# A two-layer graph network: the second layer norm and the last product put two steps later, the statistics aggregated earlier within a step, and each PSUM bank of a seed copied on its own

## The reference

```
h  = max(layernorm(x), 0)
mask = adj > 0
hm[b,j] = sum_k mask[b,j,k] * relu(h[b,j] @ W1a + (h[b,j] - h[b,k]) @ W1b + b1)
x  = x + hm @ W2 + deg * b2
h  = max(layernorm(x), 0)
x  = x + (adj @ h) @ W^T
```

## Time and profile before

| | |
|---|---|
| median of 3 runs | 913.4 us |
| profiled execution | 911.69 us, span 909.7 us |
| TensorE busy | 842.6 us, 93% |
| VectorE busy | 851.5 us, 94% |
| ScalarE busy | 761.9 us, 84% |
| GpSimd busy | 614.1 us, 68% |
| mean granted TensorE clock | 0.994 |

### The profile page before, as it was taken

One profiled execution on the slowest core, in us unless ns is written; L12 is line 12 of the kernel. 1 busy time (PEld: TensorE's weight loads), 2 busy tenths in 40 slices (PEclk: granted clock), 3 DMA queues, 4 the chain that ended last, 5 costly groups with the idle time before them and its releaser, 6 DMA issues.

```text
span 909.7 us, 26109 instructions
## 1 busy us (share of the span) xinstructions
PE 842.6 (93%) x8242; PEld 718.0 (79%) x8243; DVE 851.5 (94%) x2908; ACT 761.9 (84%) x1728; POOL 614.1 (68%) x1164
## 2 busy tenths in 40 slices
PE   3768999999999999999999999999999999999995
PEld 1447888888888888888888888888888888888884
DVE  6989999999999999999999999999999999999994
ACT  4858888888888888888888888888888888888883
POOL 0956677667766776777677667766776677667763
PEclk9999999999999999999999999999999999999998
DMA  9700000000000000000000000000000000000000
GB/s 344 272 1 2 14 13 19 19 19 8 19 19 19 14 19 20 10 16 19 19 13 20 18 19 8 19 19 19 14 19 20 19 7 19 19 19 14 13 8 15
DMA packets 26699, 27.50 MB, mean 30 GB/s; under 512 B 3520, under 2 KB 24512, under 8 KB 25536
## 3 DMA queue, kind: packets, MB, share of 16 engines
q1 hardware_dynamic: 25488, 25.37, 8.2%
q10 hardware_dynamic: 1072, 0.43, 0.2%
HBM read 21.59 MB, written 4.19 MB: 28 GB/s over the span
## 4 chain that ended last, share of the span: by engine, by line
DVE 52%; PE 19%; issue 16%; ACT 9%; DMA 1%; POOL 1%; SPq 0%; DVEq 0%; ACTq 0%; POOLq 0%
DVE acc L808 31%; PE ring L400 10%; DVE onehot_space L794 7%; ACT ring L561 5%; DVE onehot_row L851 4%; DVE PQ L725 3%; PE prep L465 2%; PE prep L457 2%; DVE stats L865 2%; ACT row_space L604 1%; DVE x_all L861 1%; DMA x_all<-x_nbf_dram 1%; PE prep L463 1%; DVE mv L836 1%; DVE owner L845 1%
## 5 line engine op out<-in xcount | busy, mean ns | idle before, releaser
L808 DVE SCALAR_TENSOR_TENSOR acc<-ring,acc 128x384 f32<-128x384 f32 x896 | 490.3, 547 | 27.7 <-PE ring L400 26.8
L561 ACT COPY ring<-P 128x768 f32<-128x768 f32 x512 | 403.9, 811 | 59.0 <-DVE acc L808 47.7
L400 PE MATMUL ring<-PQ,onehot_space 128*128 128x192 f16 x4096 | 412.5, 247 | 32.5 <-ACT ring L561 19.9
L400 PEld LDWEIGHTS ring<-PQ,onehot_space 128*128 128x128 f16 x4096 | 319.6, 98 | 97.4 <-ACT ring L561 50.0
L918 POOL TENSOR_TENSOR row_space<-row_space 128x192 f32<-128x192 f32 x256 | 151.8, 593 | 125.7 <-ACT row_space L604 115.6
L904 POOL TENSOR_SCALAR start<-P,spare 128x192 f32<-128x192 f32 x128 | 120.0, 938 | 96.5 <-ACT P L618 95.7
L794 DVE TENSOR_SCALAR onehot_space<-mask_all 128x512 f16<-128x512 f16 x512 | 155.1, 305 | 0.0
L566 ACT ACTIVATE h<-x_all,shift,rstd 128x64 f32<-128x64 f32 x128 | 55.5, 434 | 60.0 <-POOL shift L936 60.0
L428 PE MATMUL ring<-PQ,owner 128*128 128x384 f16 (+1 forms) x512 | 93.9, 306 | 0.0
L400 PE MATMUL ring<-PQ,onehot_row 128*128 128x192 f16 x768 | 84.3, 246 | 1.6 <-DVE onehot_row L851 1.6
L604 ACT ACTIVATE row_space<-ring 128x576 f32<-128x576 f32 x128 | 82.4, 644 | 0.7 <-PE ring L400 0.7
(11 more groups left out here) (138 smaller groups left out, 1434.0 us busy)
## 6 DMA issues: line engine op xcount, KB each, us to landing
onehot_space<-adj_kbj_dram SPq DMA_DIRECT2D x8, 1024.0 KB, 17.8
adj_again<-adj_kbj_dram SPq DMA_DIRECT2D x128, 64.0 KB, 2.0
x_all<-x_nbf_dram SPq DMA_DIRECT2D x8, 512.0 KB, 18.5
out_dram<-x_all SPq DMA_DIRECT2D x32, 128.0 KB, 1.9
consts<-consts_dram SPq DMA_DIRECT2D x1, 192.0 KB, 2.5
scratch<-w1a_dram ACTq DMA_DIRECT2D x2, 48.0 KB, 4.2
scratch<-w1b_dram ACTq DMA_DIRECT2D x2, 48.0 KB, 6.9
scratch<-b_dram ACTq DMA_DIRECT2D x1, 96.0 KB, 10.0
```

The source lines that it names most:

```text
L400: last = nc.tensor.matmul(to, hot(s), parts[:, part, H:2 * H], start=False, stop=(part == 1), skip_group_check=True)
L561: return nc.scalar.copy(slots[to], src.unsqueeze(1).unsqueeze(1).broadcast_to([N, BANKS, PER_BANK, H]))
L808: return nc.vector.scalar_tensor_tensor(sums, slots[to][:, bank_], 0.0, start[:, :, :] if first else sums, ALU.max, ALU.subtract if first ...
```

## The change

Five things are changed.

- Layer 1's normalisation: `norm2` is gone. At the end of every step b (place `i == 4`) ScalarE normalises graph b-5, so the first graph of a pair at an odd step and the second at the next even step, one step later each than the statistics' step, or more. `h2` gets a second copy for each pair.
- The aggregation of a pair (L500) goes from odd step b for b-5 to odd step b for b-7, and the last product and addition (L468, L872) from b-6 to b-8 at even steps. `TAIL` becomes 7, and the counts of `transposes` and `mixes` follow. SyncE's reload waits for the aggregation two steps later.
- `bn_aggr` (L836) is issued after the first bank of chunk 0 and ahead of the one-hots, no longer after the second bank.
- The seed is two copies of 128x384, one for each bank, each with its own increment of `seeded`. The first waits for `half_summed` of the chunk that held the place, the second for `summed`.
- TensorE waits for `seeded` ahead of each bank's four products.

```diff
-            return (u - 5) % BODY, (b - 5) // BODY if isinstance(b, int) else t - 1 if u < 5 else t
+            return (u - 7) % BODY, (b - 7) // BODY if isinstance(b, int) else t - 1 if u < 7 else t
...
-                    sp.wait_ge(transposed, transposes(b + 5))
+                    sp.wait_ge(transposed, transposes(b + 7))
...
-                            pe.wait_ge(seeded, b * REGULAR + i + 1)
                             for bank_ in range(BANKS):
+                                pe.wait_ge(seeded, (b * REGULAR + i) * BANKS + bank_ + 1)
...
-                        if u % 2 and exists(b - 7):
-                            pe.wait_ge(y_ready, pairs(b, u, t, -7))
+                        if u % 2 and exists(b - 9):
+                            pe.wait_ge(y_ready, pairs(b, u, t, -9))
...
-                        if u % 2 and exists(b - 5):
-                            pe.wait_ge(h2_ready, b - 3)
+                        if u % 2 and exists(b - 7):
+                            pe.wait_ge(h2_ready, b - 5)
...
-            def seed(to, src):
+            def seed(to, src, bank_):
...
-                return nc.scalar.copy(slots[to], src.unsqueeze(1).unsqueeze(1).broadcast_to([N, BANKS, PER_BANK, H]))
+                return nc.scalar.copy(slots[to][:, bank_], src.unsqueeze(1).broadcast_to([N, PER_BANK, H]))
...
-                        if i in (0, 1) and exists(b - 1):
-                            act.wait_ge(summed, b * REGULAR - 1 + i)
...
-                        if i == 3:
-                            act.wait_ge(summed, b * REGULAR + 1)
-                        seed(place(u, i), P[:, u % 2, :]).then_inc(seeded, 1)
+                        for bank_, consumed in enumerate((half_summed, summed)):
+                            if i in (0, 1) and exists(b - 1):
+                                act.wait_ge(consumed, b * REGULAR - 1 + i)
+                            if i == 3:
+                                act.wait_ge(consumed, b * REGULAR + 1)
+                            seed(place(u, i), P[:, u % 2, :], bank_).then_inc(seeded, 1)
...
-                    if i == 1 and u % 2 and exists(b - 5):
-                        norm2(b, u, t, 1)
...
-                    if i == 4 and u % 2 == 0 and exists(b - 4):
-
-                        wait_apart(act, norm2_ready, pairs(b, u, t, -4))
-                        if exists(b - 6):
-                            act.wait_ge(transposed, transposes(b - 1))
-                        norm2(b, u, t, 0)
+                    if i == 4 and exists(b - 5):
+
+                        wait_apart(act, norm2_ready, pairs(b, u, t, -5 if u % 2 else -6))
+                        if exists(b - 9):
+                            act.wait_ge(transposed, transposes(b - 2 if u % 2 else b - 3))
+                        k, g = (u - 5) // 2 % 2, (u - 5) % 2
+                        nc.scalar.activation(h2[:, k, 2 * g, :], x_all[:, b - 5, :], ACT.Relu, bias=shift2[:, k, g:g + 1],
+                                             scale=rstd2[:, k, g:g + 1]).then_inc(h2_ready, 1)
...
                         consume(u, place(u, i), 0, i == 0).then_inc(half_summed, 1)
+                    if i == 0 and u % 2 == 0 and exists(b - 4):
+                        wait_apart(dve, stats2_ready, pairs(b, u, t, -4))
+                        for g in range(2):
+                            last = nc.vector.bn_aggr(mv[:, (u - 4) // 2 % 2, g, :], stats2[:, g, :])
+                        last.then_inc(mv_ready, 1)
                     if i < REGULAR:
                         prepare(b, u, i)
...
-                    if i == 4 and u % 2 == 0 and exists(b - 6):
+                    if i == 4 and u % 2 == 0 and exists(b - 8):
```

More of the change, by code:

```diff
@@ L161, in gnn_kernel @@
         shift2 = sb("shift2", [N, 2, 2])
-        h2 = sb("h2", [N, 3, F])
-        h2_padded = (h2[:, 0:2, :], h2[:, 1:3, :])
+        h2 = sb("h2", [N, 2, 3, F])
+        h2_padded = [(h2[:, k, 0:2, :], h2[:, k, 1:3, :]) for k in range(2)]
         ring = ctx.enter_context(nc.psum_tensor("ring", [N, RING, BANKS, 512], F32))
@@ L250, in gnn_kernel @@
         stored = sem("stored")
-        HEAD, TAIL = 3, 5
+        HEAD, TAIL = 3, 7
         LATE = PARTS - 1
@@ L295, in agg_at @@
         def agg_at(b, u, t):
-            return (u - 5) % BODY, (b - 5) // BODY if isinstance(b, int) else t - 1 if u < 5 else t
+            return (u - 7) % BODY, (b - 7) // BODY if isinstance(b, int) else t - 1 if u < 7 else t
         def transposes(step):
-            return step + 2 if isinstance(step, int) and step > B + 1 else step + 3
+            return B + 4 + (step - B - 1) // 2 if isinstance(step, int) and step > B + 1 else step + 3
         def mixes(step):
-            return step + 1 if isinstance(step, int) and step > B + 2 else step + 2
+            return B + 4 + (step - B - 2) // 2 if isinstance(step, int) and step > B + 2 else step + 2
         def pairs(b, u, t, d):
@@ L465, in step @@
                                 last = nc.tensor.matmul(out_ps[:, g, :], hmT[g], w2a[:, :], start=False, stop=True, skip_group_check=True)
-                        if u % 2 == 0 and exists(b - 6):
+                        if u % 2 == 0 and exists(b - 8):
                             pe.wait_ge(even_T_ready, pairs(b, u, t, -2))
@@ L499, in step @@
                                 pe.wait_ge(adj_again_in[at + g], times * 16 + 16)
-                                last = nc.tensor.matmul(agg_ps, h2_padded[g], adj_again[:, at + g, :], start=(g == 0), stop=(g == 1))
+                                last = nc.tensor.matmul(agg_ps, h2_padded[(u - 7) // 2 % 2][g], adj_again[:, at + g, :], start=(g == 0), stop=(g == 1))
                         if last:
@@ L587, in step @@
                         nc.scalar.copy(h1T[:, :], h1T_ps).then_inc(h1T_ready, 1)
-                    if i == 0 and u % 2 == 0 and (exists(b - 2) or exists(b - 6)):
+                    if i == 0 and u % 2 == 0 and (exists(b - 2) or exists(b - 8)):
                         act.wait_ge(transposed, transposes(b - 1))
-                        if exists(b - 4) or exists(b - 8):
+                        if exists(b - 4) or exists(b - 10):
                             act.wait_ge(mixed, mixes(b - 1))
-                        parts = slice(0 if exists(b - 2) else 1, 2 if exists(b - 6) else 1)
+                        parts = slice(0 if exists(b - 2) else 1, 2 if exists(b - 8) else 1)
                         nc.scalar.copy(sums_T[:, parts, :], sums_T_ps[:, parts, :]).then_inc(even_T_ready, 1)
@@ L638, in step @@
                             wait_apart(act, loop_summed, first + k + 1)
-                            seed(place(u, CHUNKS), P[:, u % 2, :]).then_inc(loop_seeded, 1)
+                            seed(place(u, CHUNKS), P[:, u % 2, :], 0)
+                            seed(place(u, CHUNKS), P[:, u % 2, :], 1).then_inc(loop_seeded, 1)
                         wait_apart(act, loop_summed, first + n + 1)
@@ L673, in _ @@
             nc.vector.memset(ones_h[:, :], 1.0)
-            nc.vector.memset(h2[:, 1, :], 0.0)
+            nc.vector.memset(h2[:, :, 1, :], 0.0)
             nc.vector.memset(row_space[:, 0, 0, H:H + F], 0.0)
@@ L832, in step @@
                         consume(u, place(u, i), 1, False).then_inc(summed, 1)
-                    if i == 0 and u % 2 == 0 and exists(b - 4):
-                        wait_apart(dve, stats2_ready, pairs(b, u, t, -4))
-                        for g in range(2):
-                            last = nc.vector.bn_aggr(mv[:, (u - 4) // 2 % 2, g, :], stats2[:, g, :])
-                        last.then_inc(mv_ready, 1)
                     if i == 0 and exists(b + 1):
@@ L870, in step @@
                             dve.wait_ge(p_ready, b + 2)
-                        pair = bass.ds(b - 6, 2)
+                        pair = bass.ds(b - 8, 2)
                         nc.vector.tensor_tensor(x_all[:, pair, :], x_all[:, pair, :], out_ps, ALU.add).then_inc(y_ready, 1)
```

4 lines of the change are left out of this document (removed).

## The result

The changed kernel takes 863.4 us, the median of 4 runs (858.9 to 867.0), beside 913.3 (912.8 to 913.5) for the one before: a ratio of 0.945, 95% interval 0.941 to 0.950. In a second set of runs it took 866.1 (863.4 to 870.3), beside 912.5. The forecast was 881.5 with a range from 867 to 905: the sign was right, the size too small by about a third (32 us of 50). The kernel's own times now spread over 8 us, where those of before lay within 1 us (within 2 us in the later sets of seven runs).

What follows compares the result with a forecast made beforehand. VectorE was taken as the bound, waiting for the odd graph's chunk 2: 911.7 - 32.6 + 0.7 = 879.8, plus 1.7 for the median, 881.5 us. Own range 868 to 895; 867 to 905 with rival 1 and some of 3.

Steps and rivals of the forecast that it cites:

- VectorE bounds the kernel, and its wait for the odd graph's chunk 2 is the gain: VectorE, 96.02 of 100 us busy, is the bound; its 0.44 us wait for TensorE's gather there can be given back.
- Rival 1: Seeds and gathers: the wait is shortened, not ended, only 0.21 a pair gained, 13.4 us, giving 899; chance 0.13.
- rival 2: ScalarE becomes the bound because half seeds don't overlap: slower, +26 us at the upper end, 940; chance 0.06.
- rival 4: Nothing changes: the gather waits for something else than seeds, or the wait only moves; 913 to 914, chance 0.03.
- VectorE stands still in one place worth naming, so a pair gives 0.51, 32.6 us in all: VectorE ahead of the odd graph's chunk 2: ending this one wait gives 0.51 in each of 64 pairs.
- Half seeds alone 0.43 at chunk 2, the move 0.21: TensorE's gathers: chunk 1's 0.43 earlier by half seeds, 0.21 more without waiting for chunk 2's seed; chunk 2's 0.64 earlier.
- The split's cost: ScalarE: splitting a seed costs about 0.005 us each, 0.04 a pair, up to 0.27 each; hidden at the low end.
- TensorE's waits, the aggregation, SyncE: TensorE's four more waits a graph, VectorE's earlier aggregation and SyncE's later reload: taken to cost or gain nothing.
- The end, +0.7: Last steps: +1.1 for a longer last round against at least 0.33 saved; net +0.7, bounds -0.5 and +2.3.
- VectorE and GpSimd, no change in the middle: VectorE's fp16 instructions lengthened by GpSimd: no net change taken, two meetings more or less (13 us) as range.
- rival 3: VectorE and GpSimd meet more often: eight meetings +26 us, 907, or 932 by the skill's rule; chance 0.06, half slower.
- The median is 1.7 above the profiled execution: Whole kernel: 1.7 us added to the 879.8 forecast for the profiled execution to get the median, 881.5.

Runs made afterwards that it cites:

- e9_no_reads_before: Kernel before the change, GpSimd's wide instructions in the graph loop (all but the 64-column ones) replaced by one- or two-element powers, their results left out: 887.9 us.
- e3_no_aggr: Changed kernel with the statistics aggregation back behind the second bank of chunk 0: 867.2 us, beside 866.1 for the changed kernel in the same set.
- e4_again: Changed kernel, unedited, run and traced once more: 866.1 us.
- e2_move: Kernel before with everything of the change but the half seeds, their waits, TensorE's waits for them and the earlier aggregation: 905.3 us, ratio 0.993.
- e8_bias_odd: Changed kernel with GpSimd's bias and its addition moved from the even to the odd step: 923.5 us, ratio 1.012.
- e1_split: Kernel before with only the two half seeds, their two waits and TensorE's wait for each bank: 871.5 us, ratio 0.955.

## Why the prediction was wrong

- *VectorE bounds the kernel, and its wait for the odd graph's chunk 2 is the gain*: right, as far as it goes. The distance fell from 0.79 to 0.26 in the pairs shown and from 0.76 to 0.26 in the mean, 0.50 where the sum had 0.51, and no new wait came. Rivals 1, 2 and 4 didn't occur. (Rival 1's 899 was added up wrong: 911.7 - 13.4 + 0.7 + 1.7 is 901.)
- *VectorE stands still in one place worth naming, so a pair gives 0.51, 32.6 us in all*: this is the step that failed. The price of that one wait was right; that everything else gives nothing was not. The rest of a pair fell by 0.72, 46 us. Of the missing 0.22, 0.10 lay at the odd graph's first bank, where VectorE came just in time, about 0.03 at the even graph's, and the remainder in pieces of 0.02 or less whose cause wasn't looked for. The 0.10 showed as a mean idle time of 0.03 us; the other 0.07 were lost overlap with the instruction before. That the place waits for a gather is shown by three runs: half seeds alone and the move alone each bring its distance from 0.30 to 0.20 or 0.21, and in e9_no_reads_before the idle time there opens to 0.35, for TensorE. I had counted lost overlap at chunk 2, where the idle time pointed to it, and nowhere else. A comparison of each start-to-start distance with the shortest of the same pair of instructions would have found them.
- *Half seeds alone 0.43 at chunk 2, the move 0.21*: the 0.43 and 0.21 by which the gather should come earlier; measured 0.30 and 0.19 of VectorE's distance there. With half seeds alone two things differed from the estimate: seeds were 0.41 and not 0.37 apart, and ScalarE still waited for the shift, 37.3 us in 64 times. How much each cost wasn't tested.
- *The split's cost*: 0.005 taken, 0.09 measured, inside the bounds and 18 times the value taken. By the account it cost no time, since ScalarE had 1.7 us of idle time in a pair to give and VectorE waits for hardly any gather now. ScalarE has little left: 97% busy.
- *TensorE's waits, the aggregation, SyncE*: for the aggregation nothing, as e3_no_aggr shows. The other two weren't tested apart; VectorE has no wait left in the middle that could come from them.
- *The end, +0.7*: measured -0.4, from the last graph's first bank to the end of the span 20.1 us and before 20.5. The last round is longer, as said: the last normalisation ends at 858.32, the last addition at 861.91, 3.6 us where it was 2.3. The steps before it are shorter by more than I had counted. The size isn't firm: e4_again, the same kernel, has 19.4, which would make it -1.1, and e2_move has 20.6.

```profile
857.88 0.44 ACT L618 ACTIVATE h<-x_all,shift,rstd 128x64 f32<-128x64 f32 x1
...
861.62 0.29 DVE L868 TENSOR_TENSOR x_all<-x_all,prep 128x128 f32<-128x128 f32 x1 [2.47 <-PE prep L468]
```

- *VectorE and GpSimd, no change in the middle*: by chance right for the mean, 0.38 and 0.39 us of holds. The price of a meeting was not: up to 0.36 us, where the row of before showed 0.1 and rival 3 worked out 0.3 as a mean from the length of a row sum. So the range for it, two meetings more or less, 13 us, was far too narrow for what the same work does in e8_bias_odd.
- *The median is 1.7 above the profiled execution*: that held for before alone. After, it is 3.7 below. With times that spread over 8 us, one profiled execution doesn't give the median.

The sum with measured terms: 911.7 - 46 - 0.4 + 0.6 (holds) = 866, beside 867.0 of the profiled execution. The 0.22 a pair that were missed (about 14 us) and the 5.4 us between 1.7 above and 3.7 below make up the 18 us by which the forecast was too high; the end and the holds nearly cancel.

## What to carry to other kernels

Read the bound engine by distances from start to start, not by idle time: an instruction that becomes ready just as the one before it ends costs its overlap, 0.07 to 0.09 us here, and shows hardly any wait; compare each distance with the shortest of its kind. When two edits are measured one by one in a tightly timed loop, split the period into the waits and the lengthened instructions before adding them up, and count a lengthened instruction only where the next one starts later. Here 41 and 7 us made 46 to 50, while without holds half seeds gave 22.5 us and the move on top of them 22.0. And when an engine's instructions take two different lengths for the same shape, look at what another engine started just before: three waits in a pair, no work saved, gave another 10 us.

## What the runs showed of the hardware

- An fp16 instruction of VectorE that starts shortly after a wide one of GpSimd is held. Behind a 128x192 sum of two inputs (0.59 us long) the comparison takes 0.32 to 0.34 us too long when it starts 0.06 to 0.09 us after it, 0.20 at 0.20, 0.12 at 0.28, 0.09 at 0.32 and nothing from 0.40 on, so that the hold ends 0.40 us after the sum's start; 512-column one-hots are held 0.17 at 0.30, 0.10 at 0.36 and nothing at 0.48. Behind the second fp16 part (0.55) it is 0.36 at 0.05, 0.20 at 0.2, 0.10 at 0.32 and nothing at 0.42. Behind the 128x192 product by a column (L904, about 0.94) it is 0.12 to 0.16 at 0.14 to 0.26 and nothing from 0.34 on. Behind powers of one or two elements (0.54 to 0.77 long) it is 0.04 at the most, and mostly nothing. The consuming instructions, which read PSUM and one tile of SBUF, were never held (0.52 to 0.56 us in all traces).
- The one that starts first isn't held. In e1_split the comparison started from 0.03 us ahead to 0.02 behind the row sum 52 times: it took 0.22 us, and the sum 0.65 to 0.68 and not 0.59.
- The Trainium skill, "SBUF — State Buffer", section "Who interferes with whom", says that the second of two such instructions is blocked until the first ends, and that a VectorE instruction with at most one SBUF input outside the fast modes isn't touched. The second half agrees with the consuming instructions. The first doesn't quite: the hold ended some 0.4 us after the start of an instruction that the profile gives 0.59 us, and GpSimd's spans are rough, so whether the profile or the rule is off stays open.
- The same program spread over 7 to 8 us in two sets of four runs; the two traces differ in the number of long pairs. With the row sums' or all wide reads gone the spread was 0.6 to 1.5 us, with them timed 4.7. The granted TensorE clock doesn't explain it: the fastest run of the changed kernel, 858.9 us, had 0.978, the slowest of that set, 867.0, had 0.991.
